# A transformer layer with eight experts: the whole tiles' rows loaded a second time as blocks of 32 features and turned by VectorE instead of TensorE, and the last scatters and the padding spread over tiles

## The reference

```python
def ref(x):
    x = layernorm(x + attention(x))              # 16 heads of 8, key 0 partly taken out
    w, sel = phi_routing(x @ gate_w.T)           # two experts a token, with weights
    out = 0
    for e in range(8):
        h = silu(x @ w1[e].T) * (x @ w3[e].T)    # 128 -> 512
        out += wte[:, e:e+1] * (h @ w2[e].T)     # 512 -> 128
    return layernorm(x + out)
```

## Time and profile before

| what | value |
|---|---|
| median of 3 runs | 1306.14 us (1305.42 to 1310.01) |
| profiled execution: its own time | 1305.69 us |
| profiled execution: span from first to last instruction | 1304.0 us |
| busy: PE, DVE, ACT, POOL | 96%, 70%, 63%, 52% of the span |
| mean granted TensorE clock | 0.990 |

### The profile page before, as it was taken

One profiled execution on the slowest core, in us unless ns is written; L12 is line 12 of the kernel. 1 busy time (PEld: TensorE's weight loads), 2 busy tenths in 40 slices (PEclk: granted clock), 3 DMA queues, 4 the chain that ended last, 5 costly groups with the idle time before them and its releaser, 6 DMA issues.

```text
span 1304.0 us, 22210 instructions
## 1 busy us (share of the span) xinstructions
PE 1248.6 (96%) x7135; PEld 636.7 (49%) x7135; DVE 919.2 (70%) x1543; ACT 815.4 (63%) x1652; POOL 681.4 (52%) x983
## 2 busy tenths in 40 slices
PE   5999999999999999999999999999898999999996
PEld 2333333333333333333333333258897999999962
DVE  7888888989888889898898999843333443333334
ACT  1677777777777777777777777774443444444636
POOL 5215546666566575665665755465535333333335
PEclk8999999999999999999999999999999999999999
DMA  5322222232222232223222223231113111111146
GB/s 174 102 68 87 72 62 82 86 97 75 83 84 85 69 94 73 96 75 93 80 85 70 87 78 113 92 92 53 50 50 92 48 51 51 49 46 40 42 141 258
DMA packets 79378, 108.32 MB, mean 83 GB/s; under 512 B 15379, under 2 KB 55959, under 8 KB 79264
## 3 DMA queue, kind: packets, MB, share of 16 engines
q1 hardware_dynamic: 69904, 87.58, 22.1%
q0 software_dynamic: 8688, 18.14, 4.2%
q10 hardware_dynamic: 672, 1.18, 0.3%
HBM read 70.34 MB, written 36.44 MB: 82 GB/s over the span
## 4 chain that ended last, share of the span: by engine, by line
PE 85%; DVE 6%; DMA 2%; issue 2%; ACT 2%; another core or an unknown queue 1%; SPq 1%; POOL 1%; ACTq 0%; POOLq 0%; DVEq 0%
PE acc_ps L509 18%; PE ring_ps L497 16%; PE mx_ps L486 15%; PE ring_ps L625 10%; PE mx_ps L609 9%; PE mx_ps L599 8%; DVE rowmax_sb L871 4%; PE ring_ps L550 2%; PE ring_ps L542 2%; PE mx_ps L660 1%; PE ring_ps L526 1%; PE ring_ps L588 1%; PE ring_ps L524 1%; PE ring_ps L517 1%
## 5 line engine op out<-in xcount | busy, mean ns | idle before, releaser
L871 DVE TENSOR_REDUCE rowmax_sb<-mx_ps 128x2 f32<-128x1024 f32 x512 | 604.5, 1213 | 84.0 <-PE mx_ps L486 82.2
L682 ACT ACTIVATE probs_sb<-ring_ps 128x512 f32<-128x512 f32 x1024 | 551.9, 598 | 77.4 <-PE ring_ps L497 58.9
L497 PE MATMUL ring_ps<-region_sb 74*128 74x512 bf16 x1024 | 351.6, 381 | 6.6 <-ACT prefix_sb L727 2.7
L486 PE MATMUL mx_ps<-region_sb 72*128 72x512 bf16 x1024 | 306.1, 380 | 10.0 <-DVE rowmax_sb L871 4.0
L509 PE MATMUL acc_ps<-probs_sb,values_sb 128*32 128x512 f32 x2048 | 273.1, 606 | 0.0
L1412 POOL DMA_INDIRECT y_d<-probs_sb,values_sb x135 | 132.3, 980 | 222.7 <-DVE probs_sb L1154 194.0
L497 PEld LDWEIGHTS ring_ps<-region_sb 74*128 74x128 bf16 x1024 | 99.8, 98 | 210.8 <-ACT probs_sb L682 96.9
L785 ACT ACTIVATE xT_sb<-region_sb 128x512 f32 x78 | 49.1, 630 | 194.3 <-PE mx_ps L609 172.9
L486 PEld LDWEIGHTS mx_ps<-region_sb 72*128 72x128 bf16 x1024 | 95.3, 98 | 121.2 <-issue 24.3
L1343 POOL DMA_INDIRECT rows_d<-sent_sb,pos_sb x128 | 126.1, 985 | 47.9 <-issue 47.9
L1154 DVE SCALAR_TENSOR_TENSOR probs_sb<-ring_ps,values_sb 128x128 f32<-128x128 f32 x135 | 42.1, 347 | 154.1 <-PE ring_ps L625 139.2
(11 more groups left out here) (177 smaller groups left out, 1166.8 us busy)
## 6 DMA issues: line engine op xcount, KB each, us to landing
region_sb<-parts_d SPq DMA_DIRECT2D x372, 96.0 KB
probs_sb<-y_d SPq DMA_DIRECT2D x32, 256.0 KB, 5.1
values_sb<-rows_d SPq DMA_DIRECT2D x57, 132.0 KB
parts_d<-q_parts_sb SPq DMA_DIRECT2D x16, 384.0 KB, 2.6
parts_d<-k_parts_sb SPq DMA_DIRECT2D x16, 384.0 KB, 2.9
xT_sb<-xT SPq DMA_DIRECT2D x16, 256.0 KB, 3.1
x_sb<-x SPq DMA_DIRECT2D x16, 256.0 KB
out<-probs_sb SPq DMA_DIRECT2D x16, 256.0 KB, 4.2
```

Of the source, the lines that this page charges most:

```text
L486: last = nc.tensor.matmul(mx_ps[n % 2][:, i, :], QS[b % 2][0:KR, h, P * c:P * (c + 1)], KS[b % 2][0:KR, h, :], start=True, stop=True)
L497: nc.tensor.matmul(bank, KS[b % 2][0:KR + MR, h, P * c:P * (c + 1)], QS[b % 2][0:KR + MR, h, :], start=True, stop=True).then_inc(s_ring_re ...
L682: nc.scalar.activation(PT[u % 2][:, i // QC, i % QC, :], ring_bank("st", u, i), ACT.Exp, scale=SCALE).then_inc(s_ring_done, 1)
L871: V.tensor_reduce(rowmax[u % 2][:, 2 * k:2 * k + 2], mx_ps[n % 2][:, :, :], axis=AXX, op=ALU.max, negate=True).then_inc(s_mx_done, 1)
```

## The change

Three things change.

1. The rows of whole tiles are loaded twice. Besides the load into `XG`, from which DVE and POOL read row, weight and destination, four DMAs per tile (`load_blocks`) bring the rows into a block layout: partition `32 i + s` gets, for each group `j` of 32 rows, the 32 features from `32 i` on of row `32 j + s`. That is 256 pieces of 128 B in each DMA, and 1024 in each tile. DVE's transpose works in blocks of 32x32; applied to this layout it gives the same `XGT` (`turn_rows`, one instruction a tile). The transposes on PE and the copy on ACT stay for small tiles alone. There are four block buffers; SP loads the blocks of tile `t` when tile `t - 4` has been turned, and behind them the rows of tile `t - 2`.
2. The scatters of the last two sequences, four at a time in tiles 6 and 9 and two at a time in tiles 20 to 23 before, are issued one a tile, in tiles 6 to 13 and 20 to 27. `send_x` of the last sequence moves from tile 11 to 17, its `count_rows` from 17 to 18.
3. The eight padding stores, issued in one go at SP's tile 27 before, are issued one a tile from there on, with 128 rows each instead of 256.

```diff
+            def load_blocks(t):
+                if t >= BRING:
+                    sp.wait_ge(s_turned, t - BRING + 1)
+                elif t == BRING - 1:
+                    sp.wait_ge(s_parts_stored[1], 16 * NB)
+                row = first_row(t)
+                for i in range(P // VW):
+                    sp.dma_start(XB[t % BRING][VW * i:VW * (i + 1), :].rearrange("s (j r) -> s j r", r=VW),
+                                 rows_d[bass.ds(row, TK), VW * i:VW * (i + 1)].rearrange("(j s) r -> s j r", s=VW))\
+                      .then_inc(s_xb_in[t % BRING], 16)
...
             for t in range(TILES):
-                if t == RING:
+                if t == BRING:
                     load_weights(UNITS - 1, s_w2, (W2, w2T))
-                elif t == RING + 21:
-                    pad_ends()
+                elif RING + 21 <= t < RING + 21 + E:
+                    pad_end(t - RING - 21)
...
+                if t < FULL:
+                    load_blocks(t)
+                for n in range(t - 2 if t <= FULL else t, t - 1 if t < FULL else t + 1):
+                    if is_tile(n):
+                        load_rows(n)
...
             def tile_up(t):
-                pe.wait_ge(s_xgt, t + 1)
+                if t < FULL:
+                    pe.wait_ge(s_turned, t + 1)
+                else:
+                    pe.wait_ge(s_xgt, t - FULL + 1)
...
                 beside(t, 0)
-                if is_tile(t + 1):
-                    tile_in(t + 1)
+                if FULL <= t + 1 < TILES:
+                    small_tile_in(t + 1)
...
+            def turn_rows(t):
+                dve.wait_ge(*blocks_in(t))
+                if t == 0:
+                    dve.wait_ge(s_parts_stored[1], 16 * NB)
+                if t >= 2:
+                    dve.wait_ge(s_lin, t - 1)
+                V.transpose(XGT[t % 2][:, :], XB[t % BRING]).then_inc(s_turned, 1)
+
+            turn_rows(0)
             for t in range(TILES + 1):
-                tail(t)
+                if t == 0:
+                    tail(t)
+                if t + 1 < FULL:
+                    turn_rows(t + 1)
+                if t > 0:
+                    tail(t)
                 if is_tile(t - 1):
+                    dve.wait_ge(*rows_in(t - 1))
                     dve.wait_ge(s_y_ready, t)
...
+            def chunk(n):
+                return n // QC, range(n % QC, n % QC + 1)
...
-                elif t in (6, 9):
-                    scatter(b - 1, (t - 6) // 3)
...
-                elif t == 11:
+                elif t == 17:
                     send_x(b)
-                elif t == 17:
+                elif t == 18:
                     count_rows(b)
-                elif t in (20, 21, 22, 23):
-                    scatter(b, (t - 20) // 2, range(t % 2 * 2, t % 2 * 2 + 2))
+                elif 20 <= t < 20 + 2 * QC:
+                    scatter(b, *chunk(t - 20))
+                if 6 <= t < 6 + 2 * QC:
+                    scatter(b - 1, *chunk(t - 6))
```

More of the change, by code:

```diff
@@ L174, in layer @@
         XGT = [parts_flat[1][:, n * TK:(n + 1) * TK] for n in range(2)]
+        XB = [row_blocks[:, 0:TK], row_blocks[:, TK:2 * TK],
+              values_flat[:, RING * HALVES * ROW:RING * HALVES * ROW + TK], parts_flat[1][:, 2 * TK:3 * TK]]
+        BRING = len(XB)
         at = 0
@@ L227, in layer @@
         s_xg = [sem(f"xg_loaded{n}") for n in range(RING)]
-        s_xgt_ready, s_xgt = sem("xgt_ready"), sem("xgt_drained")
+        s_xb_in = [sem(f"row_blocks_loaded{n}") for n in range(BRING)]
+        s_turned, s_xgt_ready, s_xgt = sem("rows_turned"), sem("xgt_ready"), sem("xgt_drained")
         s_up, s_lin, s_silu, s_h = sem("up_ready"), sem("lin_ready"), sem("silu_done"), sem("h_done")
@@ L308, in rows_in, with blocks_in @@
             return s_xg[t % RING], 16 * (t // RING + 1)
+        def blocks_in(t):
+            return s_xb_in[t % BRING], 16 * (P // VW) * (t // BRING + 1)
         def rows_out(t):
@@ L409, in _, with pad_end @@
                     load_weights(p - 1, s_w2, (W2, w2T))
-            def pad_ends():
+            def pad_end(e):
                 sp.wait_ge(s_ends, 1)
[L413 to L416, removed]
+                end = sp.value_load(end_i[0:1, e:e + 1], min_val=0, max_val=E * REGION - TK)
+                sp.dma_start(rows_d[bass.ds(end, P), :], padrow[:, :]).then_inc(s_pad, 16)
             load_x(NB - 1)
@@ L421, in _, with first_row, load_rows @@
             sp.wait_ge(s_pv_ready, UNITS - NG)
+            def first_row(t):
+                return sp.value_load(row0_i[0:1, t:t + 1], min_val=0, max_val=E * REGION + (E - 1) * TK)
+            def load_blocks(t):
[8 more added lines that the diff above has]
+                      .then_inc(s_xb_in[t % BRING], 16)
+            def load_rows(t):
+                if t >= RING:
+                    sp.wait_ge(*rows_out(t - RING))
+                row = first_row(t)
+                sp.dma_start(XG[t % RING][:, 0:halves(t), :], rows_d[bass.ds(row, P * halves(t)), :]
+                             .rearrange("(w p) r -> p w r", p=P)).then_inc(s_xg[t % RING], 16)
             for t in range(TILES):
-                if t == RING:
+                if t == BRING:
                     load_weights(UNITS - 1, s_w2, (W2, w2T))
-                elif t == RING + 21:
-                    pad_ends()
+                elif RING + 21 <= t < RING + 21 + E:
+                    pad_end(t - RING - 21)
                 elif t == FIRST:
@@ L786, in copy_weights, with small_tile_in @@
                       .then_inc(s_w_copied, 1)
-            def tile_in(t):
-                act.wait_ge(s_xgt_ready, t + 1)
+            def small_tile_in(t):
+                act.wait_ge(s_xgt_ready, t - FULL + 1)
                 n = P * halves(t)
```

15 lines of the change are left out of this document (4 added, 11 removed).

## The result

| kernel | median | runs | profiled execution, span |
|---|---|---|---|
| before | 1308.08 us | 1305.42 to 1316.78, 4 runs | 1304.0 us |
| changed | 1295.27 us | 1291.07 to 1298.3, 4 runs | 1293.7 us |

A forecast was written before the change was run, and what follows sets the result against it. PE was taken as the bound, busy for the whole steady stretch of the tile stage. From 1305.69 us, -12.5 - 0.3 - 12.5 + 1.2 = -24.1 gave 1281.6, said as 1282; forecast 1276 to 1288, range up to 1308.

The forecast's parts named there:

- Transposes, -12.5: In the tile stage, 57 tiles lose two PE transposes of 0.22 us each, 12.5 us, all on the path.
- The handover: Between DVE's product and the down projection, no longer hidden by transposes: loss taken as nothing, 3.4 us kept for the range.
- DVE's turn: In each tile, behind the product: 0.35 us, at most 0.69, in DVE's idle time; DVE from 38% to 46%, cost 0.
- The start, -0.3: First up projection: 0.8 us gained without ACT's copy, 0.5 lost because W2 is issued later, at about 863.4.
- SP and DMA engines: In each tile, SP needs 4.5 us of 5.24 and the DMA engines 1.8 to 3.2 us; both fit.
- my two prices: DMA engine time for a packet in the block loads: 12 ns or 34 ns, 0.8 or 2.3 us a tile.
- Rival D: SP's queue and DMA rings: block loads become the bound, 1299 us at 1.16 a DMA, 1379 at 1.44; chance 0.19.
- It is hidden either way: Block loads' DMA time in each tile costs nothing, since four tiles (21 us) lie between a load's release and its use.
- Send and count, +1.2: Send moved to tile 17, count to 18: DVE waits some 3.5 us near tile 19 and PE loses 1.2.
- Scatters and padding spread, -12.5: Long tiles beside POOL's scatter bursts: late releases go if bursts cause them, 12.5 us back, bounds 0 and 12.5.
- no wait of L625 above 0.5 us except near tile 19: Sign that the forecast is right: the down projection (L625) waits no longer than 0.5 us, except near tile 19.
- Rival B: Tile stage: late releases aren't from POOL's bursts, so waits stay: 1294 us, or 1288 with half of them; chance 0.23.

The follow-up runs named there:

- condition B: Label for the later sets of runs, on three other chips than the first set; the kernel before takes 1292.3 to 1292.7 us beside them.
- A: Label for the first profiles of both kernels and the first set of runs; the kernel before takes 1306.8 us (median of 16) beside that set.
- e1_spread_only: Kernel before with only scatters, send and padding placed as in the changed kernel, no block loads and no turn: 1297.5 us, ratio 0.9915.
- e0_again: The changed kernel once more, unaltered: 1292.45 us, ratio 0.9874.
- e3_send_back: Changed kernel with the last sequence's send back at tile 11 and the count at tile 17: 1294.09 us, ratio 0.9879.
- e2_blocks_only: Changed kernel with scatters, send and padding placed as before, only the blocks and the turn new: 1302.77 us, ratio 0.9966.
- e7_burst0_spread: Changed kernel with the eight row scatters at the start issued one a tile in tiles 0 to 7, the next eight in 8 to 15: 1282.99 us, ratio 0.993.
- b0_before: The kernel before once more, unaltered, for a second profile: 1292.61 us (one run).
- e4_dose_before: Kernel before with extra row scatters to unread tensors in single steady tiles, in doses of 1, 2, 4 and 8: 1293.7 us, one run.
- e11_blocks_twice: Changed kernel with each block set loaded a second time into an unread buffer, nine DMAs a tile instead of five: 1328.58 us, ratio 1.0286.

## Why the prediction was right, and where not

*Transposes, -12.5.* Right: 5.461 to 5.246 is 0.215 a tile, 12.3 in all. The handover lost nothing, and the 3.4 us that I kept for it in the range weren't needed.

*DVE's turn.* 0.43 us, not 0.35: half the columns took more than half the time. Hidden as said. DVE is at 45% against a forecast of 46%.

*The start, -0.3.* The gain of 0.8 came as 0.7. W2 was issued at 871.03, 4.5 us behind the start of the first up projection, where 5.6 was forecast. In condition B that cost nothing (tile 1 has 0.46 too much against 0.47 before). In A tile 1 lost 2.6 us more than before; whether W2, the first burst beside block loads, or both did it is open.

*SP and DMA engines.* 3.8 us of SP's time against 4.5, share 0.34 inside 0.3 to 0.6. From 0.17 of 5.46 to 0.34 of 5.25 is 0.86 us more on 16 engines for 1088 small packets: 12.6 ns each (estimate from two shares), the lower of my two prices. That is about a third of the 34 ns of a row of 528 B, but per byte half as much again. The Trainium skill (DMA: Bandwidth & Descriptors, Specifications) has pieces under 512 B read, modified and written, and below full rate. The rate agrees, 10 B/ns against 15.5; whether reading and writing back is behind it, no run here shows. Rival D was wrong at five DMAs a tile, and its mechanism, SP's issue time, real at nine.

*"It is hidden either way".* This is the step that failed: the block loads' cost beyond SP and DMA share, which the sum had at nothing. In A they brought late waits with them. From `e1_spread_only` to `e0_again`, both with the new placing, only blocks and turn are new, and the medians fall by 5.0 us where the shorter tiles (12.3) and the start (0.7) bring 13.0; the tile stages fall by 4.9 where the shorter tiles alone bring 12.3. Some 7 to 8 us are missing. In the tile stage of `e0_again` 1.2 of them are the waits in tiles 7 and 20, and nearly all the rest is late waits of 0.1 to 2.3 us in tiles 0, 1, 8, 12 to 14 and 23 to 29. Why block loads bring late waits in A stays open.

*Send and count, +1.2.* Measured 1.15, with DVE waiting 3.65 where 3.5 was forecast. What I didn't see is that the move also kept POOL's catching up away from the row scatters, which was worth 4.6 us in tile 15 of the profile of `e3_send_back`. Tile 7's 0.48 I had missed: DVE waits 1.9 us there for POOL's residual sum, behind the turn; `e1_spread_only`, with the same scatters and no turn, loses nothing in that tile.

*Scatters and padding spread, -12.5.* With the send this term was -11.3. The new placing brought 9.3 us by the medians of A without block loads (`e1_spread_only`) and 10.3 beside them (from `e2_blocks_only` to `e0_again`), and 14.1 in the profiles' tile stages: about right in A. In the profile of the changed kernel, 14.5 us of late waits went and 7 came back as smaller ones (tiles 1, 8, 14, 24, 25, 27, 28), by the step above. The sign "no wait of L625 above 0.5 us except near tile 19" failed there, with waits of about 1 us.

*Rival B* named the right total, but by luck. Its mechanism, waits that don't come from the bursts, is against `e1_spread_only`: tiles 11 and 24 lost their waits with the placing. But its reason, a burst that is harmless elsewhere, was a good one: in B the same burst does nothing, so a burst isn't enough by itself, and no dose was measured in A.

*The reference itself.* 12.5 of the 24 us forecast hung on waits that the same program has in one condition and not in another (391.3 and 376.4 us of tile stage). In B the changed kernel's work gains the transposes and the start alone, and the ratio of `e7_burst0_spread` is 0.993. That the ratio and the total came out inside the range thus hangs on the condition as well as on the mechanism. What makes the condition is open, the chip included: the profiles show the same POOL issues and packets in both, and the doses could only be run in B.

## What to carry to other kernels

Before a gain is booked for removing waits, look at a second execution, on another chip if there is one: a wait whose releaser the profile can't name may be gone there, while a stretch without such waits comes back to 0.01 us. Spread descriptor work of one engine over the tiles, and look for bursts that arise by themselves where an engine catches up after a long operation. A load that is hidden by bandwidth still has a price on the queue that issues it: count issues and register loads a tile, and leave room below the tile's time.

## What the runs showed of the hardware

- The kernel before lost 14.5 us to late waits in one profile and nothing in a second; with the doses it lost nothing in three more (376.44 us of tile stage in each of the four, to the hundredth). The attention stage took 812.7 us in the first and 806.9 to 807.5 in the others.
- In A late waits came to 14.5 us without block loads and 17.6 with them (`e2_blocks_only`), and after spreading to 0.3 us without block loads and 6 to 7 with them (sums over the tiles of one profile each, two for the last).
- A burst of eight scatters cost tile 11 4.9 us in the first profile of before and nothing in `b0_before`; one of sixteen cost nothing in `e4_dose_before`.
- PE ran at 1.2 GHz around 30 us in all profiles but the first one of before: 5 to 11 us at the first score. In `e2_blocks_only` and `e11_blocks_twice` the row of the granted clock says 1.00 there, and two matmuls take 1.06 us all the same: of clock and durations, the durations are the surer.
- A set of four block DMAs, 256 pieces of 128 B each, takes SP 1.8 us in the median of the changed kernel's 57 sets (1.4 to 3.6), and a packet of 128 B about 12.6 ns of one DMA engine (estimate, above).
- DVE's transpose in blocks of 32x32 took 0.43 us for 128x256 and 0.69 for 128x512.
